# A kernel of cross attention and feed-forward: the first batch's low halves on POOL, and transfers reordered at start, middle and end

## The reference

```python
x = x + autocorrelation(layernorm(x), ctx, ctx)
x = x + ffn(layernorm(x))

# autocorrelation(Q, K, V), along the 512 positions, per column:
corr = ifft(fft(q) * conj(fft(k))).real
w, idx = top_k(corr, 12); w = softmax(w)
out = sum_i w_i * v[min(idx_i + pos, L - 1)]

# ffn: 16 experts of rank 16 on top of one matrix
out = x @ W.T + bias + sum_e (x @ A_e.T) @ B_e.T * coeffs_e * scales_e
```

## Time and profile before

| | us |
|---|---|
| median of 3 runs | 2785.59 (2785.28 to 2786.66) |
| profiled execution, time | 2788.0 |
| its span, first to last instruction | 2786.0 |
| PE busy | 2647.7 (95%) |
| POOL busy | 2165.1 (78%) |
| DVE busy | 1839.6 (66%) |
| ACT busy | 1097.0 (39%) |

### The profile page before, as it was taken

How to read it: one execution, slowest core, us unless ns; L and a number is a source line. 1 busy time by engine, 2 the same in 40 slices (tenths; PEclk the granted TensorE clock), 3 DMA queues, 4 the chain that set the end, 5 groups by cost and what they waited for, 6 DMA issues and landing times.

```text
span 2786.0 us, 39716 instructions
## 1 busy us (share of the span) xinstructions
PE 2647.7 (95%) x14112; PEld 1706.3 (61%) x14112; DVE 1839.6 (66%) x4710; ACT 1097.0 (39%) x1873; POOL 2165.1 (78%) x1558
## 2 busy tenths in 40 slices
PE   5999855899999999999999999999999999999998
PEld 4666644566666666666666666666666666664443
DVE  5888889766776677666776677667766577644200
ACT  4777734533343343433444344443433244211000
POOL 5899988777897799877897799877897789645222
PEclk8999978899999999999999999999999999999999
DMA  8499985845676566945776476845775476548953
GB/s 311 113 267 263 247 233 130 239 145 203 234 235 207 192 225 224 262 138 189 248 236 211 174 245 221 248 154 186 249 207 166 168 246 225 165 147 303 293 171 113
DMA packets 444390, 587.30 MB, mean 211 GB/s; under 512 B 216992, under 2 KB 343072, under 8 KB 426528
## 3 DMA queue, kind: packets, MB, share of 16 engines
q1 hardware_dynamic: 444192, 584.76, 66.1%
HBM read 383.35 MB, written 151.00 MB: 192 GB/s over the span
## 4 chain that ended last, share of the span: by engine, by line
PE 79%; POOL 6%; DMA 5%; DVE 5%; SPq 2%; issue 2%; ACT 1%; POOLq 0%; DVEq 0%; ACTq 0%
PE f_ps L781 14%; PE f_ps L785 14%; PE f_ps L783 14%; PE a_ps L710 10%; PE a_ps L668 10%; PE a_ps L746 7%; PE a_ps L761 3%; PE a_ps L762 3%; PE a_ps L723 2%; DVE f_rowlo L1308 2%; POOL p_lo L1135 1%; DMA p_hi_t<-p_hi 1%; SPq L516 1%; DMA out_dram<-f_x1p 1%; DMA x_scratch<-a_rows 1%
## 5 line engine op out<-in xcount | busy, mean ns | idle before, releaser
L781 PE MATMUL f_ps<-f_whi,f_hhi 128*128 128x512 f16 x2048 | 776.9, 379 | 3.9 <-DMA f_hlo<-h_scratch 2.4
L785 PE MATMUL f_ps<-f_whi,f_hlo 128*128 128x512 f16 x2048 | 776.9, 379 | 0.0
L783 PE MATMUL f_ps<-f_wlo,f_hhi 128*128 128x512 f16 x2048 | 776.7, 379 | 0.0
L865 ACT ACTIVATE a_side<-a_ps 128x256 f32<-128x256 f32 (+1 forms) x192 | 87.1, 454 | 961.4 <-PE a_ps L746 726.9
L710 PE MATMUL a_ps<-a_w_lag,lags 128*128 128x256 f16 x3072 | 356.2, 273 | 1.3 <-DVE a_tf L1167 1.3
L785 PEld LDWEIGHTS f_ps<-f_whi,f_hlo 128*128 128x128 f16 x2048 | 200.5, 98 | 242.1 <-issue 0.8
L783 PEld LDWEIGHTS f_ps<-f_wlo,f_hhi 128*128 128x128 f16 x2048 | 200.5, 98 | 224.8 <-issue 0.8
L710 PEld LDWEIGHTS a_ps<-a_w_lag,lags 128*128 128x128 f16 x3072 | 300.2, 98 | 60.2 <-issue 4.6
L781 PEld LDWEIGHTS f_ps<-f_whi,f_hhi 128*128 128x128 f16 x2048 | 200.5, 98 | 212.5 <-issue 5.0
L1042 POOL TENSOR_TENSOR a_prod<-a_prod,a_tf 128x512 f32<-128x512 f32 x128 | 160.5, 1275 | 215.5 <-DVE a_tf L1167 215.5
L1042 POOL TENSOR_TENSOR a_zv<-a_zv,a_tw 128x512 f32<-128x512 f32 x128 | 187.1, 1480 | 132.8 <-DVE a_tf L1167 132.7
(11 more groups left out here) (130 smaller groups left out, 5324.8 us busy)
## 6 DMA issues: line engine op xcount, KB each, us to landing
f_whi<-whi_scratch SPq DMA_DIRECT2D x128, 512.0 KB, 5.4
f_wlo<-wlo_scratch SPq DMA_DIRECT2D x128, 512.0 KB, 6.6
a_rows<-in_x_dram SPq DMA_DIRECT2D x62, 1024.0 KB, 8.4
vs<-in_ctx_dram SPq DMA_DIRECT2D x64, 512.0 KB, 7.6
xs<-in_x_dram SPq DMA_DIRECT2D x64, 512.0 KB, 3.6
parts_scratch<-a_so SPq DMA_DIRECT2D x64, 512.0 KB, 4.7
x_scratch<-a_rows SPq DMA_DIRECT2D x32, 1024.0 KB, 5.1
f_x1p<-x_scratch SPq DMA_DIRECT2D x32, 1024.0 KB, 6.2
```

Source lines behind the costliest of these rows:

```text
L781: nc.tensor.matmul(f_ps[:, t, :], h_hi[q][:, kq, rows_t], w_hi[u % WR][:, :, kq, :], start=(k == 0), stop=False)
L783: nc.tensor.matmul(f_ps[:, t, :], h_hi[q][:, kq, rows_t], w_lo[u % WR][:, :, kq, :], start=False, stop=False)
L785: mm = nc.tensor.matmul(f_ps[:, t, :], h_lo[q][:, kq, rows_t], w_hi[u % WR][:, :, kq, :], start=False, stop=(k == DB - 1))
L865: return nc.scalar.activation(out, source, ACT.Copy, **how)
```

## The change

Six edits. (1) The low half of the four row tiles of batch 0 is computed by POOL, in windows 10 to 13, after POOL's additions for the attention; the later batches stay on DVE. (2) The low half of the last prepared tile (tile 15) is computed in window 10 and not at the end of window 9, on POOL behind the row addition; SP's transpose and store of it move to window 10 too. (3) In a window SP issues the row store and the next attention load ahead of the prepared tiles' stores and transposes. (4) Before the windows, two tiles of x rows are loaded ahead of the values, and `fold` after the first chunk of x. (5) The last output group is stored in four pieces of 256 KB, each after its own addition. (6) The final wait counts these.

```diff
@@ store_group
+                if g == 4 * BATCH - 1:
+                    for t in range(TB):
+                        sp.wait_ge(y_added, TB * g + t + 1)
+                        sp.dma_start(out[b, t * T:(t + 1) * T, cols], x1p[:, t, :]).then_inc(out_out, 16)
+                    return
                 sp.wait_ge(y_added, TB * (g + 1))
                 sp.dma_start(out[b, :, cols].rearrange("(i p) d -> p i d", p=T), x1p[:, :, :]).then_inc(out_out, 16)
@@ before the windows, SP
-            shared.load_v(sp, 0)
-            shared.load_fold(sp)
             load_first_rows(0, rows[0][:, :])
             load_first_rows(1, rows[1][:, :])
+            shared.load_v(sp, 0)
             load_first_rows(2, w_sb[:, 0, :])
             load_first_rows(3, w_sb[:, 1, :])
             shared.load_x(sp, 0)
+            shared.load_fold(sp)
             shared.load_matrices(sp)
@@ windows, SP
+                if r is not None:
+                    store_x1(w, r)
+                    if r % TB < TB - 1:
+                        load_attn(r + 1, True)
                 if made:
                     store_high(2 * w - 4)
                     turn_low(2 * w - 4)
                     load_tile(2 * w - 4 + PW)
                     turn_high(2 * w - 3)
                     store_low(2 * w - 4)
-                if r is not None:
-                    store_x1(w, r)
-                    if r % TB < TB - 1:
-                        load_attn(r + 1, True)
...
                 if made:
                     store_high(2 * w - 3)
+                if 1 < w <= PREPARED:
                     turn_low(2 * w - 3)
                     load_tile(2 * w - 3 + PW)
                     store_low(2 * w - 3)
+                if w == PREPARED + 2:
+                    turn_low(OT - 1)
+                    store_low(OT - 1)
...
-            sp.wait_ge(out_out, 16 * 4 * BATCH)
+            sp.wait_ge(out_out, 16 * (4 * BATCH - 1 + TB))
@@ POOL
+            def row_low(w, r):
+                pool.wait_ge(hi_done, r + 1)
+                at_least(pool, h_out, 32 * r)
+                nc.gpsimd.tensor_tensor(row_lo[:, :], rows[w % 2][:, :], row_hi[:, :], ALU.subtract).then_inc(lo_done, 1)
...
                 if 1 <= w <= N:
                     add_lower(w - 1)
+                if row_tile(w - 1) is not None and row_tile(w - 1) < TB:
+                    row_low(w - 1, row_tile(w - 1))
                 if r is not None:
                     add_row(w, r)
+                if w == PREPARED + 2:
+                    tile_low(OT - 1)
                 if 1 < w <= PREPARED + 1:
                     tile_low(2 * w - 4)
                 fold_queries(w + 2)
                 fold_values(w + 2)
-                if 1 < w <= PREPARED + 1:
+                if 1 < w <= PREPARED:
                     tile_low(2 * w - 3)
@@ DVE
-                if row_tile(w - 1) is not None:
+                if row_tile(w - 1) is not None and row_tile(w - 1) >= TB:
                     row_low(w - 1, row_tile(w - 1))
```

## The result

The changed kernel takes 2774.41 us (median of 6 runs, 2772.07 to 2776.99) against 2786.12 us for the kernel before beside it: ratio 0.9957, 95% interval [0.9945, 0.997], 12 us less. The profiled execution took 2776.99 us with a span of 2775.2, against 2788.0 and 2786.0: 10.8 us of span less.

What follows compares the result with a forecast made beforehand. TensorE was taken to bound the product windows, VectorE's stalls the chain ahead of them. Middle -13.5, start +2.5 and end -1.8 gave -12.8, so 2785.6 became 2772.8 us; range 2767 to 2778.5.

Steps and rivals of the forecast that it cites:

- The stall: Windows 10 and 12: VectorE's long low half is waiting for POOL, not computing; 15.4 us each.
- POOL's new clock: Windows 10 to 13: POOL sets them, 37.64 us for window 10, 33.61 each for 11 and 12.
- rival B: Windows 11 and 12: the row addition, statistics and queries chain sets them, not POOL; -8.8 us, 2776.8; chance 16%.
- The last tile, and the row stores: Windows 9 and 10: the tile's 4.03 us return in window 10; earlier row stores keep ACT's high half from delaying POOL.
- From low half to product: Before the first product: the 22.3 us queue behind the low half stays; product 13.8 us earlier, middle -13.5.
- rival C: Before the first product: the queue ahead of the first transpose shortens, at most 7.3 us more, 2765.5; chance 7%.
- The added 0.3 us for the clock: Ahead of the first product: 0.3 us (bounds 0 and 2) added for TensorE's granted clock after a longer idle.
- The start: First loads: later `fold` and values delay ACT's first normalising from 23.90 to 26.4; +2.5 us, bounds -1.3 and +4.0.
- The end: Last output group: only 256 KB follow the last addition instead of 1024 KB; 1.8 us gained.
- rival D: Windows 10 and 12: POOL's new instruction locks out another VectorE instruction for 15.4 us; 2802.4 us; chance 3%.

Runs made afterwards that it cites:

- moves_only: start_old with the low halves of batch 0 back on VectorE, without any wait of POOL; 2788.91 us, one run.
- let_by: start_old with batch 0's low halves back on VectorE and POOL waiting for each between `a_zu` and `a_zv`; 2756.25 us.
- pool_only: The kernel before with only the four low halves of batch 0 moved to POOL; 2773.54 us.
- start_old: The changed kernel with the old order of the first loads (values and `fold` first); 2773.59 us.
- early13: start_old with POOL's low half of row tile 3 right behind `a_prod` of window 13; 2761.36 us.
- h_first: let_by with the transposes of batch 0's first quarter issued right behind the first unit of weights; 2752.3 us.
- start_only: The kernel before with only the new order of the first loads; 2787.2 us, ratio 1.0001.
- end_only: The kernel before with only the last output group stored in four pieces and the final wait counting them; 2785.28 us, one run.
- let_by_again: The let_by kernel run once more, unchanged, as the measure for the kernels beside it; 2756.34 us.

## Why the prediction was right, step by step

- **The stall.** Right, and shown: it is VectorE's wait for POOL (moves_only lengthens it by the pitch of the added POOL instruction, let_by ends it by a wait on POOL).
- **POOL's new clock.** Right to 0.1 us: 37.63, 33.63 and 33.63 us from `a_prod` to `a_prod` against 37.64, 33.61 and 33.61, the low half's pitch 4.02 against 4.03. VectorE's multiplies ended 2.3 and 2.1 us ahead of POOL's `a_prod` of windows 12 and 13, against a margin of 2.3; rival B fell.
- **The last tile, and the row stores.** The tile's time is moved and not saved, as stated. The sentence that without the early store some 2 of 4.03 us would be lost was not tested: it supposes that the tile leaves window 9. pool_only leaves it there, and nothing is lost with the late store; no run has the tile moved and the store late. Both edits together are worth nothing that can be measured: start_old has them and the end's 1.8 us over pool_only, and is no faster.
- **From low half to product.** The queue stays, 22.8 us from the low half's end against 22.5: rival C fell for this kernel. TensorE's idle time ahead of the product was mis-sized: 7 us were to come on top of the 2.4, and it grew by 13.5, since TensorE was ready 22.2 us earlier (510.72 against 532.89) and the product came 8.65 earlier. What the prediction took as given was the largest reserve in this stage: in early13 and let_by the low half is done some 10 us sooner after the start of window 13, and h_first draws another 4 us from a shorter queue. TensorE's first matmuls of the product ran at a pitch of 0.43 us for 3.7 us, about 1.8 us lost, where before it was some 3.6 us of the same and 1.7 lost; POOL's `a_zv` of window 14 comes 10.9 us after the first product, before 10.8. The added 0.3 us for the clock was 0.1, though the idle time was 15.9 us and not 9.4.
- **The start.** Mechanism right and its steps within 0.6 us: `fold` at 19.25 (18.5), folded values at 18.8 (18.6), first matmul at 19.25 (18.7), normalising at 26.77 (26.4), so +2.87 (+2.5). The x chunk landed near 18.5 and `fold` behind it at 19.2, in the order of issue. How far it reaches the end was mis-sized. In the profiled execution it was more, 4.4 by window 1. In the time it is less: three pairs with and without it differ by 0.8 (changed kernel and start_old), 1.0 (start_only and before) and 1.8 us (let_by), each inside its own spread, and the first of them between two groups. About 1 us is likely, not shown; what takes up the other 1.5 is not settled. The varying length of the first correlation hides it in any single trace.
- **The end.** 1.85 us against 1.8 in the changed kernel's trace, and 1.8 in end_only's; the times are too coarse to show it.
- **Inherited stall (rival D).** No: with POOL busy without a break, windows 10 to 12 last what POOL's own instructions add up to, so nothing of VectorE's held them.

The sum was -12.8; the medians give -11.7, the ratio -12.0, the profiled spans -10.8. The profiled execution is the slowest of the six, and its start was slow by more than the order of loads explains.

The closeness of the total is in part luck. The start cost some 1.5 us less than its term, and the rest of the change gave 12.6 us in start_old's median where 13.5 + 1.8 = 15.3 were forecast. Its interval, 9.2 to 16.2 us, includes both, so whether something is missing is open. The traces side with the forecast: in start_old, whose first correlation took 5.41 us as in the kernel before, the first product comes 14.0 us earlier, against 13.8.

## What to carry to other kernels

When an instruction on VectorE reads two tiles in SBUF and lasts many times longer than its siblings beside an unbroken run on POOL, suspect a wait: ask what POOL does, and try a single semaphore wait on POOL before moving the work to it. Here the move was worth 12 us, and the waits with the end in pieces 30. Some 10 of the difference are not the wait's own: they come from where the last low half stands, and early13 gets them with POOL's low half too. So when work is moved, look for who waits for its end and place it first in its window, not at the end of the block that it follows. Loads that an in-order engine's early instructions need can hold a stage like those that seem to gate it: `fold`, landing at 19.2 us, moved the first normalising by 2.9, of which about 1 us is likely in the time.

## What was not expected of the hardware

- VectorE's instruction with two inputs in SBUF can be locked out over many POOL instructions, eleven of them in windows 10 and 12 (15.4 us), and one more when one more was put in (21.70 us). It got in where POOL waited for its own previous instruction, a gap of about 0.1 us. But this is the exception. In the same trace of the kernel before, 16 of the 32 low halves start in the middle of a POOL instruction whose successor follows at once. Fourteen of them get their turn right behind the running one: thirteen take 2.4 to 3.0 us, and the one beside an addition of 4.5 us takes 5.10. Only the two of windows 10 and 12 wait for more (in moves_only two of the later ones wait for two instructions, 3.8 us). A short one, between two halves of the same addition:

```profile
779.56 2.60 DVE L1308 TENSOR_TENSOR f_rowlo<-a_rows,f_rowhi 128x2048 f16<-128x2048 f32 x1
```

```profile
778.73 4.56 POOL L1042 TENSOR_TENSOR a_zu<-a_zu,a_tu 128x512 f32<-128x512 f32 x2
```

- In the four kernels that leave these low halves to VectorE without a wait on POOL (before, start_only, end_only, moves_only), all eight long ones began during POOL's addition on one partition, the two of the kernel before 0.08 us into it. In let_by, too, they begin there, and with POOL waiting behind it they take 2.8 us at most.

```profile
385.41 0.72 POOL L1042 TENSOR_TENSOR a_zu<-a_zu,last 1x256 f32<-1x256 f32 x1
```

  No run changes that instruction or the moment at which VectorE's starts beside a running POOL, so what decides between one instruction and eleven stays open. The Trainium skill ("SBUF — State Buffer", Who interferes with whom) has the loser blocked for the whole instruction of the winner; fourteen of the sixteen low halves agree with that, and the two stalls of 15.4 us do not.
- When VectorE got in, POOL paid for it: 3.20 us for a 1.27-us instruction, 4.47 for a pair of 2.50.
- The 16 equal matmuls of the first correlation took 3.72, 5.41 or 6.67 us, and two executions of one kernel (let_by and let_by_again) gave 5.41 and 6.66. TensorE had waited for POOL ahead of them. The granted clock of the changed kernel there, by stretch, is a mean between its two levels (1.2 and 2.4 GHz, 0.5 and 1 in the row), so part of each stretch ran at the lower one:

```profile
28.00:40.00 12.00, 5.99 (x24) 4.96 (x24) 2.72 (x5) 9.38 (x16) 10.78 (x9) 0.57 0.95 299
40.00:52.00 12.00, 9.09 (x33) 7.53 (x33) 6.32 (x9) 0.77 (x2) 11.70 (x11) 0.72 0.96 391
```
